# First-layer expert weights kept on chip, with a ScalarE copy per block in place of a transfer per block

## The chip, the core and the metric

The kernel runs on one core of one Trainium2 chip. The metric is the device time of one execution in microseconds (us), the median of the timed runs; lower is better. One further execution was recorded by the hardware profiler, and all rows below come from it.

## What is computed

Four layers, one after the other, on x of 64 samples x 32 tokens x 128 features, all in float32. The first one orthogonalises two matrices and adds a gated response. The second normalises the tokens and passes each through the two best of eight experts. The third passes each sample through one of eight experts, and the fourth rotates the features. The change is in the second layer, called the first expert layer here, since the one after it has experts too. Cut to what matters:

```python
# first expert layer: h_flat is [2048, 128], exp_w1 [8, 128, 512], exp_w2 [8, 512, 128]
probs = jax.nn.softmax(h_flat @ router_w, axis=-1)
gates, idx = jax.lax.top_k(probs, 2)
gates = gates / gates.sum(-1, keepdims=True)
hid = jax.nn.relu(jnp.einsum('nd,edf->nef', h_flat, exp_w1) + exp_b1)
eout = jnp.einsum('nef,efd->ned', hid, exp_w2) + exp_b2
y = jnp.einsum('ned,ne->nd', eout, combine)      # combine holds the two gates of a token
x = x + y.reshape(x.shape)
# second expert layer: one expert per sample
h = gelu(x @ Wi[expert] + bi[expert]);  o = h @ Wo[expert] + bo[expert];  y = layernorm(o + x) * gamma + beta
```

## The kernel before

Each engine runs its own instruction list, written out by hand, and waits on semaphores. The expert layers don't compute all eight experts for all tokens. The 4096 pairs of token and expert are sorted on the chip into NB1 = 39 blocks of 128 rows, each block of one expert. Which expert a block has is known only at run time: VectorE writes the table `bexi` (39 integers) and signals `places`. From then on an instruction that depends on the expert takes its address from a register, which that engine has loaded from the table (`value_load`: one load instruction and two range instructions, shown as ISA in the order of instructions).

For block b of the first expert layer:

- POOL gathers its 128 rows of h from memory into `hg` (L481, a ring of RING = 4 places; it waits until block b - 4 was transposed). From block 8 on, after every second of them, it also issues a gather `xg` for the second expert layer (L474), which waits for the one two before it. The six left over follow after block 38.
- TensorE transposes `hg` (L833), and VectorE copies the result to `hgT` (L1166).
- TensorE does the up product with the 128x512 matrix `ws[r]`, r = b mod 4 (L837, four matmuls, each in two passes). This waits for `hgT`, for the matrix (`w1_ready`) and for the hidden step of block b - 2.
- ScalarE does the bias and Relu of one half of the hidden columns (L620), VectorE that of the other half (L1174).
- TensorE does the down product with `w2`, which holds all eight experts on chip (L857). The expert is in a register.
- VectorE adds the expert's output bias, `b2blk[r]`, into `es` (L1184, two places), and SP stores `es` to memory (L364).

TensorE works staggered: in step b it does the transpose of block b + 2, the up product of b + 1 and the down product of b. VectorE does the copy of b + 2, the hidden half of b + 1 and the output add of b.

SP's queue brings the matrices in. Its step b is the store of block b, then a register load, then the transfer of the matrix of block b + 4 into `ws[r]` (L356, 256 KB), then that of the bias row, spread to all partitions (L359, 64 KB). The store waits for the output add of block b, and so do the transfers behind it.

When all blocks are stored and all x gathers have landed, POOL starts the gathers of the second expert layer (L498). That layer has NB2 = 22 blocks and uses the same ring `ws` for its matrices; `wo`, `g2r` and `be2r` stay on chip. VectorE and ScalarE hold the experts of its blocks in registers (`expert2`). They load them one by one during the late blocks of the first layer: VectorE after the output adds from block 15 on (L1160, L1199), ScalarE after hidden steps (L624).

## Time and profile before

| | |
|---|---|
| median of 3 runs | 327.73 us (327.21 to 332.39) |
| span of the profiled execution | 321.2 us |
| TensorE busy in it (matmul / weight load) | 77% / 61% |
| VectorE, ScalarE, POOL busy | 57%, 35%, 40% |
| chain that ended last | PE 53%, DVE 16%, DMA 10%, POOL 8%, issue 8% |
| ws transfers of the first expert layer (L356) | 39 of 256 KB, median 3.4 us from issue to landing |
| b2blk transfers (L359) | 39 of 64 KB, median 3.8 us |
| es stores (L364) | 39 of 64 KB, median 3.8 us |
| DMA traffic in the first expert layer | about 200 GB/s |

How to read it: the span goes from the first to the last instruction on the core; the timed runs also hold what lies around it. PE is TensorE's matmul side, PEld its weight-load side, DVE VectorE, ACT ScalarE, POOL GpSimd, SP the engine that issues most transfers (SPq: its queue). Register instructions and waits don't count as busy. In a row such as `[0.38 <-issue]` the engine was idle for 0.38 us before the instruction, and what ended that was nothing that the profile shows ("issue"), or the engine and line named. Granted clock (PEclk) is the share of TensorE's full clock that it was given. Up to about 105 us the kernel runs the first layer and the normalisation, up to 138 us it routes and sorts, from 138 to 239 us the first expert layer's blocks run, and from there the second one's.

### The profile page before, as it was taken

What the parts mean: (1) busy time and instruction counts of PE and PEld (TensorE: products, weight loads), DVE (VectorE), ACT (ScalarE), POOL (GpSimd) and SP (SyncE); (2) the same over time, 40 slices, a digit from 0 to 9 for tenths busy, and PEclk for the clock granted to TensorE, in tenths of its full rate; (3) what the DMA queues carried; (4) which work ended last, traced back from release to release, by engine and by line L of the source; (5) the groups of instructions that cost most, each with busy time, mean ns of one, the idle gap of its engine ahead of it and who ended that gap; (6) DMA issues with size and microseconds to landing.
All of it is one profiled execution on the core that took longest, in us unless ns stands there. A gap on an engine that the chain in (4) does not pass through costs nothing.

```text
span 321.2 us, 6590 instructions
## 1 busy us (share of the span) xinstructions
PE 247.4 (77%) x1630; PEld 195.3 (61%) x1630; DVE 184.2 (57%) x828; ACT 113.0 (35%) x393; POOL 129.6 (40%) x169
## 2 busy tenths in 40 slices
PE   4999999997548742888888859786843997998950
PEld 2656566445424632487778859786832886887840
DVE  1456656524989699244444525453522587897982
ACT  3343354225273313022222312221212664665640
POOL 6000000000152108465556535565347787778410
PEclk9999999955755655699999998999995999999985
DMA  5169600000050045237787775866745555656200
GB/s 140 27 168 317 177 2 0 1 2 0 0 132 0 2 131 161 30 75 210 199 204 192 205 200 144 184 200 189 201 106 152 152 150 152 171 132 161 75 24 19
DMA packets 38266, 38.42 MB, mean 120 GB/s; under 512 B 9491, under 2 KB 25909, under 8 KB 38230
## 3 DMA queue, kind: packets, MB, share of 16 engines
q1 hardware_dynamic: 32038, 26.18, 29.5%
q0 software_dynamic: 3360, 7.02, 10.8%
q10 hardware_dynamic: 2832, 4.80, 5.0%
q8 instruction: 15, 0.25, 0.3%
q14 instruction: 21, 0.17, 0.2%
HBM read 32.18 MB, written 6.19 MB: 119 GB/s over the span
## 4 chain that ended last, share of the span: by engine, by line
PE 53%; DVE 16%; DMA 10%; POOL 8%; issue 8%; ACT 2%; DVEq 0%; SPq 0%; ACTq 0%; POOLq 0%
PE bank L837 15%; PE bank L857 11%; PE bank L717 10%; DMA big<-expert_rows,xg 7%; PE bank L725 5%; POOL big L498 5%; PE bank L896 2%; PE bank L743 2%; DMA expert_rows<-es 2%; POOL ohp L451 2%; DVE x1r L1038 1%; DMA hg<-h_rows,map 1%; DVE bst L1043 1%; PE bank L893 1%; PE bank L833 1%
## 5 line engine op out<-in xcount | busy, mean ns | idle before, releaser
L837 PE MATMUL bank<-hgT,ws 128*128 128x128 f32 x488 | 68.5, 285 | 16.4 <-issue 9.9
L837 PEld LDWEIGHTS bank<-hgT,ws 128*128 128x128 f32 x488 | 61.2, 197 | 21.7 <-issue 13.4
L620 ACT ACTIVATE hid<-bank,bh 128x128 f32<-128x128 f32 x78 | 24.4, 364 | 84.4 <-PE bank L837 83.1
L481 POOL DMA_INDIRECT hg<-h_rows,map x39 | 37.0, 949 | 38.0 <-PE bank L833 30.9
L717 PE MATMUL bank<-ones 128*128 128x512 bf16 x176 | 49.2, 415 | 3.5 <-ACT trs L517 3.5
L498 POOL DMA_INDIRECT big<-expert_rows,xg x44 | 42.8, 973 | 15.0 <-issue 11.5
L857 PE MATMUL bank<-w,hid 128*128 x312 | 42.3, 279 | 0.3
L1174 DVE TENSOR_SCALAR hid<-bank,bh 128x128 f32<-128x128 f32 x78 | 23.8, 347 | 30.7 <-PE bank L837 30.6
L857 PEld LDWEIGHTS bank<-w,hid 128*128 128x128 f32 x312 | 38.6, 194 | 0.7 <-issue 0.7
L438 POOL TENSOR_SCALAR big<-x1r,rstd,nmr 128x128 f32<-128x128 f32 x8 | 3.5, 447 | 80.7 <-DVE nmr L1053 80.7
L717 PEld LDWEIGHTS bank<-ones 128*128 128x128 bf16 x176 | 18.9, 119 | 20.8 <-issue 5.9
L725 PEld LDWEIGHTS bank<-Q 128*128 128x128 f32 x128 | 19.3, 210 | 18.1 <-DVE Q L981 10.6
L648 ACT ACTIVATE hid<-bank,bh 128x128 f32<-128x128 f32 x88 | 25.2, 369 | 8.0 <-PE bank L837 7.5
L569 ACT ACTIVATE gsn<-bank 128x1 f32<-128x1 f32 x64 | 11.0, 171 | 43.5 <-PE bank L725 42.1
L896 PE MATMUL bank<-wo,hid 128*128 x176 | 25.5, 288 | 0.0
L474 POOL DMA_INDIRECT xg<-x_rows,map x22 | 20.8, 944 | 11.6 <-DMA xg<-x_rows,map 6.1
L725 PE MATMUL bank<-Q 128*128 128x32 f32 (+31 forms) x128 | 21.1, 280 | 5.2 <-DMA Q<-in_L_cond_V_dram 3.3
L977 DVE RECIPROCAL gsr<-gsd 128x2 f32<-128x2 f32 x32 | 5.3, 165 | 32.8 <-ACT gsd L574 32.7
L896 PEld LDWEIGHTS bank<-wo,hid 128*128 128x128 f32 x176 | 21.3, 191 | 2.7
L1166 DVE COPY hgT<-bank 128x128 f32<-128x128 f32 x39 | 11.2, 287 | 15.1 <-issue 9.5
L1184 DVE TENSOR_TENSOR es<-bank,b2blk 128x128 f32<-128x128 f32 x39 | 11.4, 292 | 14.3 <-PE bank L857 12.4
L1225 DVE SCALAR_TENSOR_TENSOR x2a<-big,xg 128x128 f32<-128x128 f32 x22 | 7.7, 349 | 18.3 <-DMA big<-expert_rows,xg 18.3
(260 smaller groups left out, 363.8 us busy)
## 6 DMA issues: line engine op xcount, KB each, us to landing
ws<-in_L_cond_exp_w_dram SPq DMA_DIRECT2D x39, 256.0 KB, 3.4
ws<-in_L_cond_Wi_dram ACTq DMA_DIRECT2D x18, 256.0 KB, 3.1
b2blk<-in_L_cond_exp_b_dram SPq DMA_DIRECT2D x39, 64.0 KB, 3.8
expert_rows<-es SPq DMA_DIRECT2D x39, 64.0 KB, 3.8
out_dram<-yo SPq DMA_DIRECT2D x80, 16.0 KB
x_rows<-x1r SPq DMA_DIRECT2D x1, 1024.0 KB, 6.9
h_rows<-big SPq DMA_DIRECT2D x4, 256.0 KB, 2.4
ws<-in_L_cond_Wi_dram SPq DMA_DIRECT2D x4, 256.0 KB, 3.9
```

The lines of the kernel that those rows point to most:

```text
L474: pool.indirect_dma_start(out=xg[:, j, :], out_offset=None, in_=xdram, in_offset=bass.IndirectOffsetOnAxis(ap=map2[:, j:j + 1], axis=0)).t ...
L481: pool.indirect_dma_start(out=hg[:, b % RING, :], out_offset=None, in_=hdram, in_offset=bass.IndirectOffsetOnAxis(ap=map1[:, b:b + 1], axi ...
L498: pool.indirect_dma_start(out=eg[:, j, k, :], out_offset=None, in_=edram, in_offset=bass.IndirectOffsetOnAxis(ap=xg[:, j, C_SLOT + k:C_SLO ...
L620: last = act.activation(hid[:, u, c, :], ps[2 + u][:, c * P:(c + 1) * P], ACT.Relu, bias=bh1[:, c, b:b + 1])
L648: last = act.activation(hid[:, u, c, :], ps[2 + 2 * (c // 2) + u][:, c % 2 * P:(c % 2 + 1) * P], ACT.Gelu, bias=bh2[:, c, j:j + 1])
L717: mm(ps[bank][:], ones[:], ones[:].unsqueeze(1).to_broadcast([P, 4, P]), start=True, stop=True)
L725: mm(ps[4 * k][:, 0:R - i], Q[:, k, i:i + 1].to_broadcast([P, P]), Q[:, k, i:R], start=True, stop=True).then_inc(gs_dots, 1)
L837: last = mm(ps[2 + 2 * (c // 2) + u][:, c % 2 * P:(c % 2 + 1) * P], ws[:, w, c * P:(c + 1) * P], hgT[:, u, :], start=True, stop=True)
L857: last = mm(ps[6 + u][:, 0:D], hid[:, u, c, :], w2[:, bass.ds(e, 1), c, :], start=(c == 0), stop=(c == FC - 1))
L896: last = mm(ps[6 + u][:, 0:D], hid[:, u, c, :], wo[:, bass.ds(e, 1), c, :], start=False, stop=(c == FC - 1))
L1174: last = dve.tensor_scalar(hid[:, u, c, :], ps[4 + u][:, (c - FC // 2) * P:(c - FC // 2 + 1) * P], bh1[:, c, b:b + 1], 0.0, ALU.add, ALU.max)
L1184: dve.tensor_tensor(es[:, u, :], ps[6 + u][:, 0:D], b2blk[:, r % RING, :], ALU.add).then_inc(es_ready, 1)
```

## The change

The kernel after loads `exp_w1` of all eight experts (2 MB) into `w1` and all rows of `exp_b2`, spread over the partitions (512 KB), into `b2r`, once, on SP's queue after the other weights and ahead of `wo`. In place of the transfer per block, ScalarE copies the matrix of block b + 3 from `w1` to `ws`, right after its hidden step of block b; the first three copies come before block 0. VectorE reads the bias row straight from `b2r`. SP only stores in this stage. The expert numbers are now needed in registers of ScalarE and VectorE. They are loaded in batches: blocks 0 to 19 before the stage, 20 to 38 in the middle of it, and those of the second layer at its end (22 on VectorE, 18 on ScalarE). The register loads one by one are gone. Everything else is the same; the instructions of POOL and TensorE are unchanged.

```diff
+        w1 = sb("w1", [P, E, FF])
+        b2r = sb("b2r", [P, E, D])
-        b2blk = sb("b2blk", [P, RING, D])
...
+        def experts_in(table, first, last, engine):
+            _, es_ = nc.values_load_multi_w_load_instructions(table[0:1, first:last], engines=[engine], min_val=0, max_val=E - 1)
+            return list(es_)
+        def row_of(t, e):
+            return t[:, bass.ds(e, 1), :].rearrange("p o d -> p (o d)")
...
+            sp.dma_start(w1[:], exp_w1.rearrange("e d f -> d e f")).then_inc(ld_w1, 16)
+            sp.dma_start(b2r[:], exp_b2.partition_broadcast(P)).then_inc(ld_w1, 16)
             sp.dma_start(wo[:], Wo.rearrange("e (c p) d -> p e c d", p=P)).then_inc(ld_wo, 16)
...
-            def weights1(b, r):
-                e = sp.value_load(bexi[0:1, b:b + 1], min_val=0, max_val=E - 1)
-                if b >= RING:
-                    sp.wait_ge(up_ps, b - RING + 1)
-                sp.dma_start(ws[:, r, :], exp_w1[bass.ds(e, 1), :, :].rearrange("e d f -> (e d) f")).then_inc(w1_ready[r], 16)
-                if b >= RING:
-                    sp.wait_ge(es_ready, b - RING + 1)
-                sp.dma_start(b2blk[:, r, :],
-                             exp_b2[bass.ds(e, 1), :].rearrange("e d -> (e d)").partition_broadcast(P)).then_inc(b2_ready[r], 16)
-            def step1(b, r):
-                store(b, r)
-                if b + RING < NB1:
-                    weights1(b + RING, r)
-            sp.wait_ge(places, 1)
-            for b in range(RING):
-                weights1(b, b)
-            blocks(NB1, step1)
+            blocks(NB1, store)
...
                 last.then_inc(hidA_sb, 1)
-                if 0 <= b - FIRST2 < NB2 - RING:
-                    expert2.append(act.value_load(bex2i[0:1, RING + b - FIRST2:RING + b - FIRST2 + 1], min_val=0, max_val=E - 1))
+                if b + RING - 1 < NB1:
+                    weights1(b + RING - 1, (r + RING - 1) % RING)
+            def weights1(b, r):
+                if b >= RING:
+                    act.wait_ge(up_ps, b - RING + 1)
+                act.activation(ws[:, r, :], row_of(w1, expert1[b]), ACT.Copy).then_inc(w1_ready, 1)
...
-            blocks(NB1, hidden)
+            act.wait_ge(places, 1)
+            act.wait_ge(ld_w1, 32)
+            expert1 = experts_in(bexi, 0, 20, mybir.EngineType.Activation)
+            for b in range(RING - 1):
+                weights1(b, b)
+            for b in range(20 - RING + 1):
+                hidden(b, b % RING)
+            expert1 += experts_in(bexi, 20, NB1, mybir.EngineType.Activation)
+            for b in range(20 - RING + 1, NB1):
+                hidden(b, b % RING)
+            expert2 += experts_in(bex2i, RING, NB2, mybir.EngineType.Activation)
...
-                pe.wait_ge(w1_ready[r % RING], 16 * (b // RING + 1))
+                pe.wait_ge(w1_ready, b + 1)
...
-                dve.wait_ge(b2_ready[r % RING], 16 * (b // RING + 1))
-                dve.tensor_tensor(es[:, u, :], ps[6 + u][:, 0:D], b2blk[:, r % RING, :], ALU.add).then_inc(es_ready, 1)
+                dve.tensor_tensor(es[:, u, :], ps[6 + u][:, 0:D], row_of(b2r, expert1[b]), ALU.add).then_inc(es_ready, 1)
...
-                if 0 <= b - FIRST2 < NB2:
-                    expert2.append(expert(bex2i, b - FIRST2))
+            dve.wait_ge(ld_w1, 32)
+            expert1 = experts_in(bexi, 0, 20, mybir.EngineType.DVE)
...
-            blocks(NB1, step1)
+            for b in range(20):
+                step1(b, b % RING)
+            expert1 += experts_in(bexi, 20, NB1, mybir.EngineType.DVE)
+            for b in range(20, NB1):
+                step1(b, b % RING)
+            expert2 = experts_in(bex2i, 0, NB2, mybir.EngineType.DVE)
```

ScalarE's queue at the beginning of the stage, from the copies of the bias tables (`bh`) to the first hidden steps, before:

```order
L632 ACTIVATE bh<-bank 128x156
L633 ACTIVATE bh<-bank 128x88
L620 ACTIVATE hid<-bank,bh 128x128 x32
L624 TENSOR_LOAD bex2i
L624 ISA x2
L620 ACTIVATE hid<-bank,bh 128x128 x2
```

And after, where L611 is the hidden step and L620 the copy into the ring:

```order
L628 ACTIVATE bh<-bank 128x156
L629 ACTIVATE bh<-bank 128x88
L307 TENSOR_LOAD bexi
L307 ISA x40
L620 ISA
L620 ACTIVATE ws<-w 128x512
...
L611 ACTIVATE hid<-bank,bh 128x128 x2
L620 ISA
L620 ACTIVATE ws<-w 128x512
```

A load of 20 values with its 40 range instructions and three copies now stand between the bias tables and the first hidden step, and each hidden step (two instructions) is followed by one address instruction and one copy.

The same queue in mid stage, after: the second batch stands between the copy for block 19 and the hidden step of block 17. Before, there was nothing but hidden steps and single loads.

```order
L620 ACTIVATE ws<-w 128x512
L307 TENSOR_LOAD bexi
L307 ISA x38
L611 ACTIVATE hid<-bank,bh 128x128 x2
L620 ISA
L620 ACTIVATE ws<-w 128x512
```

Nothing of the batch's length may pass the hidden step behind it, for which TensorE's down product of block 17 waits.

VectorE's queue in mid stage, before, at a late block, with the output add (L1184), the single load (L1160), the copy of hgT (L1166) and the hidden half (L1174):

```order
L1184 TENSOR_TENSOR es<-bank,b2blk 128x128
L1160 TENSOR_LOAD bex2i
L1160 ISA x2
L1166 COPY hgT<-bank 128x128
L1174 TENSOR_SCALAR hid<-bank,bh 128x128 x2
```

And after, behind the output add of block 19:

```order
L1186 ISA
L1186 TENSOR_TENSOR es<-bank,b2r 128x128
L307 TENSOR_LOAD bexi
L307 ISA x38
L1169 COPY hgT<-bank 128x128
L1177 TENSOR_SCALAR hid<-bank,bh 128x128 x2
```

One load with 38 range instructions now stands ahead of the copy of hgT for block 22, at one place, and each output add has an address instruction ahead of it.

## Rows read from the trace of the kernel before

**Rows 1.** Timeline, ScalarE's hidden steps: start us, us, engine, line, operation [idle before <-releaser].
```profile
142.38 0.63 ACT L620 ACTIVATE hid<-bank,bh 128x128 f32<-128x128 f32 x2 [1.67 <-PE bank L837]
144.27 0.62 ACT L620 ACTIVATE hid<-bank,bh 128x128 f32<-128x128 f32 x2 [1.27 <-PE bank L837]
...
234.66 0.63 ACT L620 ACTIVATE hid<-bank,bh 128x128 f32<-128x128 f32 x2 [1.59 <-PE bank L837]
```

**Rows 2.** Timeline, a stretch without a hole, 225.4 to 227.1 us.
```profile
225.41 0.62 ACT L620 ACTIVATE hid<-bank,bh 128x128 f32<-128x128 f32 x2 [1.28 <-PE bank L837]
...
226.10 0.97 PEld L837 LDWEIGHTS bank<-hgT,ws 128*128 128x128 f32 x8
...
226.30 0.29 DVE L1184 TENSOR_TENSOR es<-bank,b2blk 128x128 f32<-128x128 f32 x1 [0.28 <-PE bank L857]
...
226.99 0.97 PEld L857 LDWEIGHTS bank<-w,hid 128*128 128x128 f32 x8
```

**Rows 3.** Waits of TensorE's load side, 138 to 238: us in total, times, longest.
```profile
PEld bank L837 <- issue: 13.4, 17, 2.7
PEld bank L837 <- DVE hgT L1166: 8.0, 7, 1.9
```

**Rows 4.** Timeline, the transfer for block 4 and its up product.
```profile
142.78 0.35 SPq L356 DMA_DIRECT2D ws<-in_L_cond_exp_w_dram  x1
...
145.62 1.13 PE L837 MATMUL bank<-hgT,ws 128*128 128x128 f32 x8 [0.38 <-issue]
```

**Rows 5.** Groups by shape, ScalarE: xcount | busy us, mean ns | idle before.
```profile
L522 ACT ACTIVATE big<-big 128x512 f32<-128x512 f32 x4 | 2.4, 615 | 0.0
```

**Rows 6.** Timeline, VectorE: output add and next copy, without and with a load.
```profile
174.51 0.29 DVE L1184 TENSOR_TENSOR es<-bank,b2blk 128x128 f32<-128x128 f32 x1 [0.28 <-PE bank L857]
174.72 0.28 DVE L1166 COPY hgT<-bank 128x128 f32<-128x128 f32 x1
...
182.40 0.29 DVE L1184 TENSOR_TENSOR es<-bank,b2blk 128x128 f32<-128x128 f32 x1 [0.28 <-PE bank L857]
...
183.10 0.29 DVE L1166 COPY hgT<-bank 128x128 f32<-128x128 f32 x1 [0.41 <-issue]
```

**Rows 7.** Timeline, VectorE and ScalarE at the beginning of either expert layer.
```profile
137.54 0.73 DVE L1166 COPY hgT<-bank 128x128 f32<-128x128 f32 x2 [5.46 <-PE bank L833]
...
139.42 1.29 ACT L620 ACTIVATE hid<-bank,bh 128x128 f32<-128x128 f32 x4 [12.94 <-PE bank L837]
...
244.62 0.35 DVE L1225 SCALAR_TENSOR_TENSOR x2a<-big,xg 128x128 f32<-128x128 f32 x1 [7.46 <-DMA big<-expert_rows,xg]
```

**Rows 8.** Timeline, the last output add and the second layer's first gather.
```profile
236.86 0.29 DVE L1184 TENSOR_TENSOR es<-bank,b2blk 128x128 f32<-128x128 f32 x1 [1.01 <-PE bank L857]
...
238.96 0.94 POOL L498 DMA_INDIRECT big<-expert_rows,xg  x1 [2.88 <-DMA expert_rows<-es]
```

**Rows 9.** Groups by shape, POOL, 138 to 238 us.
```profile
L474 POOL DMA_INDIRECT xg<-x_rows,map x22 | 20.8, 944 | 11.6 <-DMA xg<-x_rows,map 6.1 <-issue 5.5
```

**Rows 10.** Landings: es in 194:199, hg in 150:160, hg in 140:143.
```profile
DMA to landing us min/median/max: 1.7/1.7/1.7
...
DMA to landing us min/median/max: 3.9/4.1/4.3
...
DMA to landing us min/median/max: 2.5/2.5/2.5
```

**Rows 11.** Stretches: length, PE, PEld, DVE, ACT, POOL busy, PEclk, DMA share, GB/s.
```profile
192.00:194.00 2.00, 2.00 (x11) 2.00 (x11) 0.59 (x3) 0.03 (x1) 0.74 (x1) 0.50 0.18 54
194.00:199.00 5.00, 5.00 (x43) 5.00 (x42) 2.66 (x10) 1.52 (x6) 2.42 (x4) 0.90 0.58 154
```

**Rows 12.** TensorE after its longest hole: a timeline row, then rows of the chain.
```profile
190.23 1.13 PE L837 MATMUL bank<-hgT,ws 128*128 128x128 f32 x8 [2.47 <-issue]
...
191.36 1.41 PE bank L857 x8
...
192.98 1.71 PE bank L837 x8
```

More of the change, by code:

```diff
@@ L265, in cond_seq_kernel @@
         SHARED = 4
-        FIRST2 = NB1 - NB2 - 2
         RESP_BANK = (1, 2, 5, 6)
@@ L269, in cond_seq_kernel @@
         N_SMALL, N_ROWS, N_CONST, N_SIDE = len(SMALL), len(ROWS), 17 + len(IOTAS), TILES + 6
-        (ld_uv, ld_x, ld_small, ld_w2, ld_wo, ld_rows, consts, act_own, dve_own, gs_dots, gs_root, gs_norm,
+        (ld_uv, ld_x, ld_small, ld_w2, ld_w1, ld_wo, ld_rows, consts, act_own, dve_own, gs_dots, gs_root, gs_norm,
          q_ready, xt_ps, xt_sb, pooled_ps, sid_ready, side_ps, side_sb, crow_ready, fold_ps, fold_sb,
@@ L280, in cond_seq_kernel @@
          ve2_ready, rs2_ready, yn_ready, yo_ready, c_x2a, b_rr, b_stats, b_aggr, n_yg, n_yb, n_rot) = map(sem, """
-         ld_uv ld_x ld_small ld_w2 ld_wo ld_rows consts act_own dve_own gs_dots gs_root gs_norm q_ready
+         ld_uv ld_x ld_small ld_w2 ld_w1 ld_wo ld_rows consts act_own dve_own gs_dots gs_root gs_norm q_ready
          xt_ps xt_sb pooled_ps sid_ready side_ps side_sb crow_ready fold_ps fold_sb style_exp z_exp
@@ L293, in cond_seq_kernel @@
         eg_ready = [sem(f"eg_ready{i}") for i in range(RING)]
-        w1_ready = [sem(f"w1_ready{i}") for i in range(RING)]
-        b2_ready = [sem(f"b2_ready{i}") for i in range(RING)]
+        w1_ready = sem("w1_ready")
         wi_ready = [sem(f"wi_ready{i}") for i in range(RING)]
@@ L1156, in _ @@
                             ps[3][:, 2 * P:3 * P].rearrange("p (k i) -> p i k", i=TILES)).then_inc(x_row_ready, 1)
-            def expert(table, b):
-                return dve.value_load(table[0:1, b:b + 1], min_val=0, max_val=E - 1)
             def columns(b, r):
```

3 lines of the change are left out of this document (removed).

## Prediction, made before the changed kernel ran

> **What bounds the kernel now.** I started with the table of stretches and the waits, since the change touches one stage, the 39 first-layer expert blocks. ScalarE's third hidden step (block 2) starts at 142.38 and its last (block 38) at 234.66 [rows 1]. So 36 blocks take 92.28 us, 2.56 us each. Yet block 2 to block 3 takes 1.89 us (142.38 to 144.27) [rows 1]. In a late stretch TensorE's weight loads follow each other without a hole, up at 226.10, down at 226.99, 0.89 us a leg [rows 2]: two legs and a transpose of 0.11 make 1.89 us, TensorE's own pace. 36 × (2.56 − 1.89) = 24.2 us are lost to something.
>
> The waits of TensorE's load side say where: before L837, the up product, 13.4 us with no releaser that the profile shows and 8.0 us put down to VectorE's copy of hgT [rows 3]. No other wait of that size is in the list. The name of VectorE misleads. The copy just before such a stall is that of the block after next; the copy which up needs was done a block earlier. What is left of up's conditions is `w1_ready`, a DMA, and the times fit: SP issues the matrix of block 4 at 142.78, behind the store of block 0, and up of block 4 starts at 145.62 after an idle 0.38 us, 2.84 us after the issue [rows 4]. The ring has four places, but the issue waits for block 0's output add, so the transfer has less than two blocks to land in. At 1.89 us a block it does not. [...]
>
> **What goes.** 39 transfers of 256 KB and 39 of 64 KB leave the stage. What up waits for becomes a ScalarE copy from SBUF. A plain ACTIVATE of 128x512 f32 from SBUF to SBUF takes 0.615 us [rows 5]. ScalarE has 0.63 us of hidden work per block, starting 0.2 us after up ends [rows 2]; with the copy and its one address instruction it comes to about 1.3 of 1.89 us. Block b's copy is issued right after the hidden step of block b − 3, so it is done some 1.3 us after up of b − 3, and up of b starts two periods later: more than 3 us to spare. Gain: **24.2 us**, provided that nothing else then sets the pace.
>
> **What is added.** (a) One load of 2 MB and one of 512 KB before `wo`, in the first 60 us. At the table's rates it is some 10 us of transfer; it lands long before block 0 and nothing but the second layer's `wo` is behind it. Cost 0; without cover at most those 10 us.
>
> (b) Register loads: a block's expert number must be in a register of ScalarE and of VectorE. They come in batches of 20, 19 and (22 or 18): one load instruction plus two range instructions a value. The trace has single loads, on VectorE after each output add of a late block: from the start of the add to the start of the next copy 174.51 to 174.72 = 0.21 us without, 182.40 to 183.10 = 0.70 us with a load [rows 6]; 0.49 us for one load and two register instructions. How that splits is not shown. Bounds for a register instruction: nothing, and 0.118 us, since TensorE's queue gets through 16 instructions (nine matmuls, one load, six register instructions) in 1.89 us [rows 2]. I take 0.08, so the load itself is 0.33.
>
>  - Before block 0: 20 values, 0.33 + 40 × 0.08 = 3.5 us. VectorE is idle 5.46 us there and ScalarE 12.94 us, of which three copies take 1.9 [rows 7]. Hidden. Between the layers VectorE is idle 7.46 us for 22 values, 3.9 us [rows 7]. Hidden.
>  - In mid stage: 19 values, 0.33 + 38 × 0.08 = 3.4 us on each engine. On VectorE it stands ahead of the copy of hgT for block 22. In the steady rows the add starts at 226.30 and the up after next would start at 226.10 + 1.89 = 227.99; less 0.29 for the copy and 0.1 for the signal leaves 1.3 us of slack [rows 2]. Stall 2.1 us. On ScalarE it stands ahead of hidden of block 17: the hidden step shown begins at 225.41, the one before 1.89 us earlier, and the copy is handed over some 0.6 us into that, at 224.1; the step shown has to begin by 226.2 to be ready for the down product at 226.99 [rows 2]; slack 2.1, stall 1.3 us. They hit different blocks, so they add up: **3.4 us**. Behind each stall stand only hidden steps and copies, which TensorE waits for itself.
>
> (c) The end. The second layer's gathers begin when the last output store has landed (2.1 us after the last add, [rows 8]) and when all x gathers have. Six x gathers are left after block 38's h gather, and each waits for the one two before it; POOL issues at 0.944 + 0.30 us each [rows 9]. With a landing of l us the last has landed 2.4 + 4l us after the transpose of block 34. At 1.89 us a block the store has landed 14.6 us after it. A gather's landing is 4.1 us (median of a loaded stretch) and 2.5 us at its lightest [rows 10]; at 4.1 the x chain would end 4.2 us late, at 3.3 it would be 1.0, at 2.5 nothing. The stage loses two thirds of its bytes, so I take between the last two: **0.5 us**.
>
> [...]
>
> (d) TensorE's clock. [...]
>
> **Sum.** 24.2 − 3.4 − 0.5 = 20.3 us. The profiled span of 321.2 becomes 300.9; the median of the runs is 6.5 us above the span, so 327.7 becomes **307.4 us**. The second layer (from 239.0) is shifted, not changed: its preloads, its gathers and its SP queue stand as before.
>
> **Rivals.**
>  1. *Forecast*, 305 to 311 us. Chance 0.55.
>  2. *The loads hide.* If a register instruction costs next to nothing (the batch stays near 0.5 us), both are inside the slack, and the tail too: 327.7 − 24.2 = 303.5. For it: TensorE carries a load and six register instructions per block without a hole [rows 2]. Against: VectorE's 0.49 is visible. Chance 0.15.
>  3. *POOL becomes the pace.* From block 8 on it issues three gathers per two blocks, 3 × 1.244 = 3.73 of 3.78 us [rows 9]. If waiting for its semaphores stretches the pitch to 1.4 us, 31 blocks go at 2.1 instead of 1.89: 6.5 us more, 313.9. Or the store of es, double-buffered, binds: landing + 0.44 us per two blocks, which needs over 3.3 us; 1.7 at lighter load speaks against it [rows 10]. Chance 0.15.
>  4. *The change does not do what it says*: up did not wait for ws but for something that comes as late (the h gather, say). Then only part is gained, within 2%, 321.2 or more. Against: no wait before the transpose L833 in the list [rows 3]. Chance 0.05.
>  5. *Slower: register loads at full single price.* If each value costs 0.49 us also in a batch, the first batch is 9.8 − 5.46 = 4.3 us late on VectorE; mid stage 9.3 − 1.3 = 8.0 and 9.3 − 2.1 = 7.2; between the layers 10.8 − 7.46 = 3.3 [rows 6, 7, 2]. With two clock drops (2.6) and the tail (0.5) 25.9 us: 329.4. It decides from about 0.46 us a value. Against: a batch has one load instruction, not 20, and register instructions are under 0.118 on TensorE. It is 5 us off 2% slower. Chance 0.06; 0.04 are left for what I don't see.
>
> **Numbers.** The upper bound of the known terms: 0.33 + 38 × 0.118 = 4.8 us a batch, stalls 3.5 + 2.7 = 6.2, two clock drops 2.6, tail 4.2, so a gain of 11.2 and 316.5; all at once is unlikely. Range **303 to 315**, which leaves about 2 in 10 out. Two per cent is 6.6 us, about what a measurement of this kernel can tell from no change. Faster by more: cases 1 to 3 and most of the unseen, 0.88. Within: case 4, most of 5, 0.09. Slower: 0.03.
>
> **What would show it.** Right: hidden steps 1.89 us apart; no "issue" wait before up; DMA share in the stage near 0.4; last es add near 216.5; one hole of about 1.3 us at block 17 (ScalarE) and one of about 2 at block 20 to 22 (VectorE); first gather of the second layer near 219. The split of register cost is read from these holes: above 4.8 us for a batch the bound was wrong. If L833 shows waits for hg, rival 3. The prediction falls if the period stays above 2.1 us with ws copied long before.

## The result, and the profile after

| | before | after |
|---|---|---|
| median of the timed runs | 327.47 us (326.07 to 332.39, 4 runs) | 321.08 us (316.72 to 322.54, 4 runs) |
| span of the profiled execution | 321.2 us | 314.5 us |
| first to last output add of the first expert layer | 141.4 to 236.9 us | 145.3 to 228.9 us |
| ScalarE busy | 35% | 42% |

The changed kernel is faster: ratio 0.9718, 95% interval 0.9636 to 0.98. That ratio leaves out executions more than 1.5% above the fastest of their kernel, two of the changed kernel's four among them; by the medians of the table it is 0.98. The forecast was 307.4 us and a range of 303 to 315, so the direction was right and the size wrong, by 13.7 us. Of the 20.3 us forecast, the spans show 6.7 (321.2 − 314.5) and the medians 6.4.

In the code after, L843 is the up product (L837 before), L863 the down product (L857), L839 the transpose (L833), L611 the hidden step and L620 the ring copy on ScalarE, L1169 the copy of hgT, L1177 VectorE's hidden half, L1186 the output add, L307 the register loads and their range instructions.

First a table of stretches of the kernel after, with the columns of [rows 11].

```profile
150.00:160.00 10.00, 10.00 (x92) 10.00 (x91) 6.02 (x22) 6.24 (x18) 7.46 (x8) 1.00 0.39 94
160.00:170.00 10.00, 10.00 (x92) 10.00 (x92) 5.57 (x21) 6.23 (x17) 7.54 (x8) 1.00 0.40 90
170.00:180.00 10.00, 6.68 (x60) 6.50 (x59) 4.39 (x16) 3.33 (x10) 5.66 (x6) 1.00 0.30 75
180.00:190.00 10.00, 6.75 (x60) 6.51 (x59) 2.49 (x9) 4.64 (x13) 5.66 (x6) 1.00 0.25 62
190.00:200.00 10.00, 7.44 (x41) 7.44 (x42) 3.40 (x13) 2.29 (x6) 2.22 (x3) 0.66 0.10 27
200.00:210.00 10.00, 10.00 (x92) 10.00 (x91) 5.60 (x21) 5.92 (x16) 7.11 (x8) 1.00 0.32 83
```

Where nothing stands in the way, TensorE is busy 10.00 of 10.00 us, with 90 GB/s of transfers beside it. Between 170 and 200 it is not, and in 190 to 200 the granted clock averages 0.66. The waits of 138 to 230, with the columns of [rows 3], say on what:

```profile
DVE hgT L1169 <- issue: 14.7, 2, 7.7
PEld bank L843 <- DVE hgT L1169: 8.2, 2, 6.0
...
ACT hid L611 <- issue: 5.2, 1, 5.2
...
PEld bank L863 <- issue: 3.5, 1, 3.5
```

The 13.4 us of "issue" waits before up, and the seven waits of up to 1.9 us put down to hgT [rows 3], are gone. In their place stand two long waits on VectorE, one on ScalarE, and the holes that they make on TensorE: 6.0 and 2.2 us before up, 3.5 before down. The timeline shows what each engine did before. VectorE before block 0, then VectorE in mid stage, then ScalarE in mid stage and TensorE behind the two holes (columns as in [rows 1]):

```profile
132.21 0.29 DVE L1161 COPY x1r<-bank 128x128 f32<-128x128 f32 x1 [0.25 <-PE bank L831]
140.22 0.49 DVE L1169 COPY hgT<-bank 128x128 f32<-128x128 f32 x2 [7.72 <-issue]
...
184.89 0.29 DVE L1186 TENSOR_TENSOR es<-bank,b2r 128x128 f32<-128x128 f32 x1 [0.39 <-PE bank L863]
192.21 0.29 DVE L1169 COPY hgT<-bank 128x128 f32<-128x128 f32 x1 [7.03 <-issue]
...
173.25 0.63 ACT L620 ACTIVATE ws<-w 128x512 f32 x1
179.04 0.62 ACT L611 ACTIVATE hid<-bank,bh 128x128 f32<-128x128 f32 x2 [5.16 <-issue]
...
179.79 0.97 PEld L863 LDWEIGHTS bank<-w,hid 128*128 128x128 f32 x8 [3.50 <-issue]
...
192.56 2.07 PE L843 MATMUL bank<-hgT,ws 128*128 128x128 f32 x8 [5.81 <-DVE hgT L1169]
194.42 1.91 PE L863 MATMUL bank<-w,hid 128*128 x8
```

Between the two VectorE instructions of each pair, and between the two of ScalarE, the engine's queue holds one register load and its range instructions and nothing else of length. The chain of work that ended last goes through them and shows them one by one. Its columns are start us, us, what; DVEq and ACTq are the engines' sequencers. First the start of the mid-stage batch on VectorE, then a piece of the one on ScalarE:

```profile
185.19 1.68 DVEq L307
186.90 0.19 DVEq L307
187.18 0.19 DVEq L307
187.46 0.18 DVEq L307
187.73 0.18 DVEq L307
...
191.86 0.18 DVEq L307
192.21 0.30 DVE hgT L1169
```

```profile
172.85 0.51 ACTq L307
173.36 0.52 ACT ws L620
173.88 0.83 issue
174.70 0.15 ACTq L307
...
176.06 0.15 ACTq L307
176.28 0.15 ACTq L307
```

On VectorE the load of 19 values takes 1.68 us, and after it one value follows another every 0.275 us (186.90, 187.18, 187.46, 187.73): two range instructions, 0.14 us each on average. (The chain has a long row of 0.18 and a short one of 0.02 for each value, with gaps between them, so the two are not alike; the pair is what counts.) 1.7 + 19 × 0.275 = 6.9 us; 7.0 from add to copy. On ScalarE the first range instruction stands 1.85 us behind the load's start (172.85 to 174.70), and one value follows another every 0.22 us, 0.11 an instruction on average: 1.85 + 19 × 0.22 = 6.0 us of the 6.2 from 172.85 to 179.04. The forecast had 3.4 us for each batch.

**Accounts.** Before minus after, from the adds, the first gather of the second layer (238.96 and 231.06), its first x2a (244.62 and 237.33) and the end: the stage itself 95.5 − 83.6 = 11.9 us shorter; its first add 3.9 later, of which 0.5 because routing ended later in this execution (the table `map` at 131.76 in place of 131.3), about 0.3 because the first gather landed later behind it, and the rest, 3.1, because of the first batch; from last add to first gather 0.1 longer (2.2 in place of 2.1), from gather to x2a 0.6, from there to the end 0.6. 11.9 − 3.9 − 0.1 − 0.6 − 0.6 = 6.7. And within the stage: 38 periods of 1.895 us, less 0.8 at the end, where the last two adds stand 1.1 apart, are 71.2 of the 83.6. The other 12.4 are the holes of 3.5 and 6.0 us and the slow legs behind the second one: 2.07, 1.71, 1.71 and 1.02 us in the chain in place of 0.89 each, 3.0 us more.

### The profile page after: what moved, and what is told of

It is laid out like the page before. It is cut to its first block, busy times and chain, and to the rows that moved or that the text cites. A ratio compares the mean times of both kernels' runs of the same rounds, so it can differ in the third digit from the quotient of the medians.

```text
span 314.5 us, 6478 instructions
## 1 busy us (share of the span) xinstructions
PE 246.1 (78%) x1630; PEld 198.9 (63%) x1630; DVE 181.8 (58%) x828; ACT 132.9 (42%) x432; POOL 129.5 (41%) x169
## 4 chain that ended last, share of the span: by engine, by line
PE 58%; DVE 18%; DMA 6%; DVEq 6%; issue 5%; POOL 3%; ACT 2%; ACTq 1%; SPq 0%
PE bank L843 16%; PE bank L863 11%; PE bank L723 10%; DVEq L307 6%; PE bank L731 6%; DMA big<-expert_rows,xg 5%; PE bank L902 4%; PE bank L749 2%; POOL ohp L442 2%; PE bank L899 2%; DVE x1r L1044 1%; PE bank L839 1%; ACTq L307 1%; DVE bst L1049 1%; PE bank L799 1%
## 5 line engine op out<-in xcount | busy, mean ns | idle before, releaser
L843 PE MATMUL bank<-hgT,ws 128*128 128x128 f32 x488 | 70.6, 292 | 7.8 <-DVE hgT L1169 7.8
L843 PEld LDWEIGHTS bank<-hgT,ws 128*128 128x128 f32 x488 | 64.9, 207 | 8.2 <-DVE hgT L1169 8.2
L611 ACT ACTIVATE hid<-bank,bh 128x128 f32<-128x128 f32 x78 | 24.4, 364 | 49.8 <-PE bank L843 44.6
L863 PE MATMUL bank<-w,hid 128*128 x312 | 42.4, 280 | 3.3 <-ACT hid L611 3.3
L863 PEld LDWEIGHTS bank<-w,hid 128*128 128x128 f32 x312 | 39.1, 197 | 3.6 <-issue 3.5
L1177 DVE TENSOR_SCALAR hid<-bank,bh 128x128 f32<-128x128 f32 x78 | 23.8, 346 | 17.5 <-PE bank L843 17.5
L620 ACT ACTIVATE ws<-w 128x512 f32 x39 | 24.3, 628 | 6.1 <-issue 6.1
L1186 DVE TENSOR_TENSOR es<-bank,b2r 128x128 f32<-128x128 f32 x39 | 11.4, 291 | 21.7 <-PE bank L863 18.3
L1169 DVE COPY hgT<-bank 128x128 f32<-128x128 f32 x39 | 10.9, 282 | 14.7 <-issue 14.7
## 6 DMA issues: line engine op xcount, KB each, us to landing
w<-in_L_cond_exp_w_dram SPq DMA_DIRECT2D x1, 2048.0 KB, 11.2
```

The source lines that it names most:

```text
L611: last = act.activation(hid[:, u, c, :], ps[2 + u][:, c * P:(c + 1) * P], ACT.Relu, bias=bh1[:, c, b:b + 1])
L620: act.activation(ws[:, r, :], row_of(w1, expert1[b]), ACT.Copy).then_inc(w1_ready, 1)
L843: last = mm(ps[2 + 2 * (c // 2) + u][:, c % 2 * P:(c % 2 + 1) * P], ws[:, w, c * P:(c + 1) * P], hgT[:, u, :], start=True, stop=True)
L863: last = mm(ps[6 + u][:, 0:D], hid[:, u, c, :], w2[:, bass.ds(e, 1), c, :], start=(c == 0), stop=(c == FC - 1))
L1177: last = dve.tensor_scalar(hid[:, u, c, :], ps[4 + u][:, (c - FC // 2) * P:(c - FC // 2 + 1) * P], bh1[:, c, b:b + 1], 0.0, ALU.add, ALU.max)
```

## The experiments

The runs fell on four chips. On one of them the kernel before took 325.6 us, as on the chip of the result; on the three others it took 351 to 355. Ratios are therefore taken within one chip alone, and what sets these chips apart has its own part below. The time in the heading of a group is the median of the kernel before on its chip.

### First group (before: 355.17 us)

No range instructions, everything else as in the change. The table's values are clamped by VectorE when it writes them:

```diff
-            _, es_ = nc.values_load_multi_w_load_instructions(table[0:1, first:last], engines=[engine], min_val=0, max_val=E - 1)
+            _, es_ = nc.values_load_multi_w_load_instructions(table[0:1, first:last], engines=[engine], min_val=0, max_val=E - 1,
+                                                                  skip_runtime_bounds_check_because="the table is clamped to E - 1 by VectorE")
```

> The changed kernel without the two range instructions per loaded value; the batches of 20, 19 and 22 (18) values and all else stay. Theory A (the range instructions are the cost: in the changed kernel 38 of them take 5.3 us on VectorE, 185.19 + 1.68 to 192.21, and 5.7 us on ScalarE, so 0.14 to 0.15 us each, and the load instruction 1.68 and 0.51 us): a batch takes about 1.7 us on VectorE and 0.5 on ScalarE. The 3.5 us hole at the down product goes, the 6.0 us hole at the up product shrinks to 0.5 or less, the copy of hgT for block 0 starts right after its transpose, and TensorE's clock stays up: 316.7 minus (2.2 + 1.2 clock at the beginning, 3.5, 6.0 + 3.0 clock, 0.6 between the layers), plus 0.4, is about 301 us. Theory B (loading many values at once is slow whatever follows): the holes stay within 1 us of 3.5 and 6.0, and the time stays within 2 us of the changed kernel.

Single loads with range instructions, one per block on each engine, in place of the batches:

```diff
+                e = act.value_load(bexi[0:1, b:b + 1], min_val=0, max_val=E - 1)
+                act.activation(ws[:, r, :], row_of(w1, e), ACT.Copy).then_inc(w1_ready, 1)
...
+                if b + 1 < NB1:
+                    expert1.append(expert(bexi, b + 1))
+                if 0 <= b - FIRST2 < NB2:
+                    expert2.append(expert(bex2i, b - FIRST2))
```

> The changed kernel with one load per block instead of batches, range instructions kept: ScalarE loads a block's expert just ahead of the copy, VectorE after the output add of the block before; the second layer's loads stand one by one at the late blocks as in the kernel before. Theory A (a load with its two range instructions costs about 0.5 us on VectorE and is hidden as long as no more than the slack of 1.3 us is asked at a time, on ScalarE 2.1): no holes, hidden steps 1.89 us apart, last output add near 213, about 301 us. Rival (an engine's slack is used up by a load in each block, two in the late ones): the period grows to 2.0 or 2.1, 305 to 309 us, with holes before up put down to VectorE's copy.

The matrices on chip, but the bias rows again by a transfer of 64 KB per block, so that VectorE needs no expert numbers in the first expert layer:

```diff
-                dve.tensor_tensor(es[:, u, :], ps[6 + u][:, 0:D], row_of(b2r, expert1[b]), ALU.add).then_inc(es_ready, 1)
+                dve.wait_ge(b2_ready[r % RING], 16 * (b // RING + 1))
+                dve.tensor_tensor(es[:, u, :], ps[6 + u][:, 0:D], b2blk[:, r % RING, :], ALU.add).then_inc(es_ready, 1)
```

> The changed kernel with the bias rows brought in by a 64 KB transfer per block as before (b2blk, four places), so VectorE needs no expert numbers in the first layer and its batches of 20 and 19 go; ScalarE's copies and batches stay, also VectorE's batch of 22 between the layers. Theory A: the holes due to VectorE go (2.2 + 1.2 at the beginning, 6.0 + 3.0 in mid stage), the hole of 3.5 us at ScalarE's batch stays: 316.7 - 12.4 = about 304 us. Rival (the 64 KB transfers with their stores are in the way: SP's queue or the landings bind): the period stays above 2.0 us and the time above 308.

The kernel before, with the transfer of the matrix issued ahead of the store on SP's queue:

```diff
                 if b >= RING:
-                    sp.wait_ge(es_ready, b - RING + 1)
+                    store(b - RING, r)
...
-                store(b, r)
                 if b + RING < NB1:
                     weights1(b + RING, r)
+                else:
+                    store(b, r)
```

> The kernel before with one thing moved: SP issues the matrix transfer of block b + 4 as soon as block b's up product is done, ahead of the store of block b instead of behind it, some 1.6 us earlier in the steady state. Nothing is kept on chip. Theory A (TensorE waited for a transfer that was issued too late, 2.84 us ahead of its need against a landing of 3.4): the waits before the up product mostly go, period 1.9 to 2.0 us, 307 to 311 us. Rival (the DMA traffic itself binds, about 200 GB/s now and 270 at TensorE's pace): landings grow to 4.5 us or more, the period stays above 2.3, over 318 us.

| kernel | us | ratio to before, 95% | output adds, first to last |
|---|---|---|---|
| x1 no range instructions | 345.46 | 0.974, 0.9627 to 0.9854 | 142.5 to 229.8 |
| x2 single loads | 349.16 | 0.9818, 0.9724 to 0.9911 | 143.2 to 232.0 |
| x3 bias by transfer | 351.08 | 0.9833, 0.9718 to 0.9949 | 146.6 to 238.5 |
| x4 before, early issue | 351.1 | 0.9877, 0.9779 to 0.9976 | 145.4 to 241.4 |

In absolute numbers all four missed, since the chip was another. Their intervals overlap, so the times alone do not rank them; the traces say more. In x3 VectorE has no batch left, and no wait of "issue" kind before its hgT copy is in the list of 138 to 240 us, where the changed kernel has two of up to 7.7 us; ScalarE kept its batch, and its longest wait of that kind before a hidden step is 5.8 us, against 5.2. So each hole goes with the batch of its own engine. In x2, with a load in every block, the longest "issue" wait before hgT is 1.0 us: spread over the blocks, the same instructions make no long hole. x4 kept 15.2 us of "issue" waits before up, so the order on SP's queue alone doesn't bring the matrix in time.

### Second group (before: 352.92 us)

The changed kernel itself and the one without range instructions (same edits as above), on another chip:

> The changed kernel, unaltered, beside the next two, since the four runs before this one were taken where the kernel before needs 355 us instead of 327, and so don't stand beside it. Theory A (its three holes cost 13 to 16 us over x1): it lies 10 to 16 us above the run without range instructions. Theory B (the holes are made up for elsewhere): within 5 us of it.

> The changed kernel without range instructions again, beside the changed kernel. Theory A: 10 to 16 us faster than it, and about 0.92 to 0.95 of the kernel before. Theory B: less than 5 us faster.

VectorE with one load per block, also without range instructions; ScalarE keeps its batches:

```diff
+                if b + 1 < NB1:
+                    expert1.append(expert(bexi, b + 1))
...
+            def expert(table, b):
+                return experts_in(table, b, b + 1, mybir.EngineType.DVE)[0]
+            expert1, expert2 = [expert(bexi, 0)], []
-            expert1 += experts_in(bexi, 20, NB1, mybir.EngineType.DVE)
```

> As the run without range instructions, and VectorE's batches replaced by one load per block (second layer's loads one by one at the late blocks): what is left of its holes should be the load instructions of 1.68 us before block 0 (hidden), at block 20 (0.4 to 1.4 us) and between the layers (hidden). Theory A: 0.5 to 1.5 us faster than without range instructions. Rival (a single load per block, at the late ones two, costs VectorE more than it saves): 1 to 3 us slower than that.

The changed kernel with ScalarE's mid-stage batch issued twice:

```diff
             expert1 += experts_in(bexi, 20, NB1, mybir.EngineType.Activation)
+            experts_in(bexi, 20, NB1, mybir.EngineType.Activation)
```

> The changed kernel with ScalarE's mid-stage batch (one load, 38 range instructions) issued twice in a row. Theory A (the hole at the down product is the batch's length less the slack; a batch is 0.51 + 5.68 = 6.2 us): ScalarE's hidden step of block 17 begins about 11.3 us instead of 5.2 us late, and the hole before the down product is 3.5 + 6.2 = 9.7 us; VectorE's hole stays as it was. Rival (the hole has another cause, an instruction fetch or a signal): it grows by 1 us or less.

| kernel | us | ratio to before, 95% | output adds |
|---|---|---|---|
| y1 changed | 363.55 | 1.0282, 1.0208 to 1.0355 | 144.9 to 246.3 |
| y2 no range instructions | 345.69 | 0.972, 0.9602 to 0.9838 | 144.0 to 232.6 |
| y3 the same, VectorE single | 344.89 | 0.9764, 0.9693 to 0.9834 | 142.8 to 233.3 |
| y4 ScalarE's batch twice | 373.03, one run | | |

The range instructions are worth 18 us here. y1 and y4 fell on the kind of chip described below, so a part of their waits is not the batches'. The doubled batch tests the mechanism: the waits of y1, then of y4 (there the lines of TensorE are one higher), same columns as above:

```profile
ACT hid L611 <- remote: 37.2, 15, 3.3
...
PEld bank L863 <- issue: 15.7, 15, 4.7
DVE hgT L1169 <- issue: 14.8, 2, 7.7
```

```profile
PEld bank L864 <- issue: 21.6, 15, 10.4
DVE hgT L1170 <- issue: 14.4, 2, 7.7
...
ACT hid L611 <- issue: 11.2, 1, 11.2
```

ScalarE's hole becomes 11.2 us, and TensorE's longest wait before the down product goes from 4.7 to 10.4, by 5.7 us for one batch more (6.2 was expected, the batch's own length); VectorE's waits stay. So the batch is the hole.

### Third group (before: 351.61 us)

The kernel before, for its trace on such a chip; the changed kernel; the one of y3; and that one with a load per block on ScalarE too (an edit as in x2, without range instructions):

> The kernel before, for its trace. On the chips of the last two comparisons it took 352 to 355 us, on the first one 327.7, and no trace of it was taken there. If this chip is of the slower kind: theory A (signals from TensorE to the other engines come some 1.2 us late, in both expert layers) expects the first expert layer to be longer than on the first chip (first to last output add 95.7 us there) by less than the changed kernel's, since up waits for the transfer anyway: 97 to 101 us; and the second layer, from its first gather to the end, 100 to 106 us in place of 82.2. Theory B (the DMA alone is slower there) expects the issue wait before up to be above 30 us in place of 13.4 and 8.0, and the signals as fast as before. If it is of the faster kind, the rows are those known and the time is 327 us.

> The changed kernel again, beside a trace of the kernel before. On a chip where before takes 327 us: 321 us, ratio 0.97 to 0.98. On one where it takes 353: the ratio was 1.028 on one such chip; theory A (late signals add to the length of each register batch and to the start-up behind it) expects 1.02 to 1.03 again; if the result is under 1.00, the slower result was that one chip's.

> No range instructions anywhere; VectorE loads one number after each output add, ScalarE still in batches of 20 and 19. Price of range instructions (theory A): on a chip of the faster kind 14 to 17 us below the changed kernel, 304 to 308 us, which is what the prediction's sum came to with batches that hide. On a chip of the slower kind 345, as before, 16 to 19 us below changed. Rival: the rest of the forecast gain was lost to something else than the batches (the ring copies on ScalarE, signals); then not below 312 on the faster kind.

> As the kernel before it in this call, but ScalarE too loads one number before each ring copy, without range instructions, so that no batch stands in the first expert layer on either engine. A load of one value without range instructions was 0.2 us on VectorE. ScalarE then has 0.65 of hidden step, 0.2 to 0.5 of load and 0.63 of copy, at most 1.8 of 1.89 us. If the load is 0.2, the time is the same as with batches (within 1 us, since the batch of 19 values without range instructions left no hole at block 17). If a single load costs 0.5 us or more on ScalarE, its hidden steps come late and the time is 3 to 10 us longer.

Medians: z1 350.66 (one run), z2 360.73 (ratio 1.0203, 1.0055 to 1.0351), z3 348.87 (0.99, 0.9835 to 0.9966), z4 347.51 (0.99, 0.9858 to 0.9941). So the changed kernel came out slower on a second chip too, though with an interval that reaches down to 0.55%. z3 and z4 can't be told apart by these times: a single load fits into ScalarE's period as well as a batch without range instructions does. z3 was expected at 345 and 16 to 19 us below z2; it came to 3.9 us above the first number and 11.9 below z2.

### Fourth group (before: 325.58 us)

The same three kernels on a chip of the kind that the forecast was for:

> The changed kernel, as the base for the two below. If before takes 327 us here: 316 to 322 us. If it takes some 350, signals from TensorE come late in both expert layers, the period is 2.31 us in place of 1.89, and the changed kernel takes 355 to 363 us.

> The changed kernel without range instructions, batches kept. My theory (range instructions at 0.14 to 0.15 us each are the whole hole behind a batch): where before takes 327 us, the holes of 3.5 us (block 17) and 6.0 us (block 22), the late start (2.2), what the clock costs behind them (1.2 and 3.0) and 0.6 between the layers go, all but some 1.4 of the middle hole: 302 to 306 us, and the first to the last output add in 73 to 76 us. Rival (the forecast gain was lost to something else too): 308 to 314. Where before takes 350 us: 345, the adds in 87 to 89 us.

> As the one before it, but VectorE loads one value after each output add. Expected: no hole in mid stage at all, 0 to 2 us below it on a chip of the first kind, equal within 1 us (or up to 3 us above, as on the last chip) on the other.

| kernel | us | ratio to before, 95% | span | output adds |
|---|---|---|---|---|
| w1 changed | 318.69 | 0.9819, 0.9755 to 0.9883 | 317.6 | 146.1 to 231.1 |
| w2 no range instructions | 308.86 (302.8 to 310.61) | 0.9541, 0.9451 to 0.9631 | 300.6 | 142.5 to 214.9 |
| w3 the same, VectorE single | 303.42 (300.46 to 304.88) | 0.9325, 0.9228 to 0.9422 | 302.7 | 146.3 to 217.4 |

Stretches of w2, then of w3, columns as in [rows 11]:

```profile
170.00:180.00 10.00, 10.00 (x92) 10.00 (x92) 5.19 (x19) 6.23 (x18) 7.41 (x9) 1.00 0.35 90
180.00:190.00 10.00, 8.98 (x81) 8.74 (x80) 5.59 (x21) 5.09 (x14) 6.57 (x7) 1.00 0.31 82
190.00:200.00 10.00, 10.00 (x92) 10.00 (x92) 5.82 (x22) 6.10 (x17) 7.54 (x8) 1.00 0.36 93
```

```profile
180.00:190.00 10.00, 10.00 (x93) 10.00 (x92) 5.70 (x22) 6.23 (x17) 7.50 (x8) 1.00 0.36 92
```

In w2 one hole is left, behind the load of the 19 values on VectorE; the chain and the timeline of w2 there:

```profile
179.17 1.73 DVEq L307
```

```profile
PEld bank L844 <- DVE hgT L1170: 1.7, 2, 1.3
```

Without range instructions the batch is 1.73 us, against a slack forecast at 1.3. The longer of TensorE's two waits is 1.3 us; the add before this batch also began late, behind a store that landed late (`[0.79 <-DMA expert_rows<-es]`), so that not all of the 1.3 is the load's: the add came at 178.88, some 0.4 us behind its turn (1.9 us after the one at 176.59). In w3 the stage has no hole between its first and last add, and its adds take 71.1 us, the 71.2 of a stage without holes. That w3's span is 2.1 us longer than w2's all the same comes from ahead of the stage: routing ended at 134.3 in w3's execution and at 132.3 in w2's, and the first add is 3.8 later.

w1 less w2, by span: 317.6 − 300.6 = 17.0 us, made of 3.6 at the start, 12.6 in the stage (85.0 against 72.4), 0.4 to the first gather and 0.4 behind it. So in the profiled executions the whole of the missing gain was in the range instructions: the span of 300.6 us is what the sum of the prediction came to (300.9). By medians less of it is shown. w1 less w2 is 9.8 us, w1 less w3 15.3. w2's own median came out at 308.86, above the 302 to 306 expected; its profiled execution took 302.8 and the three others 307.42 to 310.61, which have no trace, so what they lost stays open. w3 has the lowest median on this chip, 22.2 us below the kernel before; y3 and y2, on a chip of the other kind, can't be told apart.

## Chips on which signals come late

On three chips the kernel before takes 351 to 355 us, and on the two of them where the changed kernel ran it is 2 to 3% slower. The traces show where. Output adds (VectorE) of before in z1, and the first gather of the second layer (POOL) in the same trace: count, ns, first and last start.

```profile
L1184 DVE TENSOR_TENSOR es<-bank,b2blk x39: 280/292/293, 142.7 to 239.2; 128x128 f32<-128x128 f32 x39
```

```profile
L498 POOL DMA_INDIRECT big<-expert_rows,xg x44: 942/954/1167, 241.3 to 325.6; - x44
```

Before's first expert layer takes 96.5 us there, nearly the 95.5 of the forecast's chip. It is the second layer that is long, from its first gather to the end of the span (348.4) 107.1 us in place of 82.2. The changed kernel (y1) has 110.2 us there, and w1 83.7, so the second layer costs both kernels about 25 us more on such a chip.

In the first expert layer the traces of these chips do not hold 1.89 us a block. ScalarE in y1, in a stretch without batches:

```profile
156.00 0.63 ACT L611 ACTIVATE hid<-bank,bh 128x128 f32<-128x128 f32 x2 [2.49 <-remote]
156.51 0.63 ACT L620 ACTIVATE ws<-w 128x512 f32 x1
157.03 0.62 ACT L611 ACTIVATE hid<-bank,bh 128x128 f32<-128x128 f32 x2
157.53 0.64 ACT L620 ACTIVATE ws<-w 128x512 f32 x1
160.68 0.63 ACT L611 ACTIVATE hid<-bank,bh 128x128 f32<-128x128 f32 x2 [2.50 <-remote]
```

Two hidden steps come close together, then nothing for 2.5 us: two blocks in 4.68 us and, over the 38 periods of y2 (144.0 to 232.6), 2.33 a block. The releaser is one that the profile can't name ("remote"). The up product that this step needs begins at 153.24. In the trace of after the hidden step follows 1.10 us behind such a start (150.78 to 151.88); here it is 2.76, so 1.7 late. VectorE's half of the same step begins at the same moment, 156.00, and TensorE has gone on to its next products at 154.13 and 155.13. Both halves wait for one signal, TensorE's, and it is read here as coming late; since the profile models the ends of matmuls, that is an inference. The next down product of TensorE then waits 0.6 to 0.8 us. With it the signs of the result can be accounted for:

 - before needs 2.56 us a block for its transfers and hides the 2.33; with the change 36 × (2.56 − 2.33) = 8.3 us remain to be gained in place of 24.2;
 - the batches cost as much as on the other kind (14.8 us of waits before hgT in y1 and w1, 5.6 and 5.1 before hidden; y1 less y2 is 12.8 us from first to last add, w1 less w2 12.6), so the sum turns negative: y1's adds take 101.4 us against 96.5 of before;
 - without range instructions the adds take 88.6 us (y2), 7.9 less than before, near the 8.3.

These sums set z1 beside y1 and y2, which ran on another chip of the same kind. On z1's own chip the adds of z3 and z4 take 92.4 and 89.8 us, some 4 and 7 less than before, so the 8.3 is not reached there. And the stage is not the whole of the loss: by span y1 is 10.2 us above z1, 4.9 of it in the stage, 2.2 ahead of it and 3.1 behind the first gather of the second layer (110.2 against 107.1), of which no row here shows the cause.

Why this happens on these chips, and only there, stays open. No experiment touched it. Theory B of z1's expectation (the DMA alone is slower) is refuted: the "issue" wait before up is 18.7 us in z1, not above 30, and with the 2.8 put down to hgT it is 21.5 us, near the 13.4 + 8.0 = 21.4 of the forecast's chip [rows 3]. Theory A missed both its ranges by little: 96.5 us for the first layer in place of 97 to 101, 107.1 for the second in place of 100 to 106.

## Why the prediction was right or wrong

**What bounds the kernel: right.** The transfer of the matrix was the 2.56 us. With it gone, the up and down products (legs) stand 0.89 us apart in the stretches without a batch, and no wait of "issue" kind before up is left. The chain after:

```profile
150.95 0.89 PE bank L843 x8
151.84 0.89 PE bank L863 x8
152.84 0.89 PE bank L843 x8
```

**What goes: right.** The ring copy takes 629 ns (36 of them, 22.6 us, with no idle before them), 615 was taken from [rows 5]. It hides. DMA share 0.39 and 0.40, "near 0.4".

**(a) The load of 2.5 MB: right.** The stages up to the table are as before but for 0.5 us. That is within what executions differ by: the table comes at 131.2 to 134.4 us in the traces with the load, and at 131.3, 131.5 and 133.9 in the three without it.

**(b) Register loads: the step that failed.** Three terms were mis-sized. The range instruction was taken as 0.08 us with 0.118 as the bound; it is 0.14 on VectorE and 0.11 on ScalarE, the mean of a pair. The bound came from TensorE's queue [rows 2] and did not hold for another engine. The load was taken as 0.33 us whatever its size: what was left of the 0.49 of a single one. It is 1.68 us for 19 or 20 values on VectorE, and 1.85 to the first range instruction on ScalarE. And the single price was split wrongly. In w3 add and copy (VectorE, timeline) stand 0.44 us apart with one load and no range instruction between them, 0.23 more than the 0.21 without [rows 6]. So of the 0.49, the load adds 0.23 and a range instruction 0.13:

```profile
161.42 0.29 DVE L1188 TENSOR_TENSOR es<-bank,b2r 128x128 f32<-128x128 f32 x1 [0.39 <-PE bank L865]
161.86 0.29 DVE L1171 COPY hgT<-bank 128x128 f32<-128x128 f32 x1 [0.15 <-issue]
```

 Had the split been 0.23 and 0.13, a batch of 19 would have come to 5.2 us with the load's size left out, and 6.6 with it. So VectorE's batch was 7.0 us in place of 3.4 and its hole 6.0 in place of 2.1; ScalarE's was 6.2, its hole 3.5 in place of 1.3. The two slacks were right. Counted as the forecast counts them, from the start of the add, and from 0.6 us into the hidden step ahead of the batch (172.73 + 0.6), they are 192.21 − 184.89 − 6.0 = 1.3 us and 179.04 − 173.33 − 3.5 = 2.2, with 1.3 and 2.1 forecast. Places and mechanism were right: blocks 17 and 22, hidden step and hgT copy, nothing else behind them. So the step that failed is the price of a batch, 3.4 us where 7.0 and 6.2 were measured.

**"Hidden" before block 0 and between the layers: wrong by the same step.** VectorE is idle 5.46 us before the stage [rows 7] and the batch took 7.7, so the first hgT copy came at 140.22 and up at 140.57 with 137.89 before; 2.2 us beyond the later end of routing (0.3 of them the later landing of the gather), and then 1.2 more in slow legs (2.08 and 1.40). The batch between the layers cost 0.6 us.

On VectorE the long load also took less than as many short ones would. A load of one value adds 0.23 us, and that of 20 values (132.50 in the chain of after) takes 1.68, 0.084 a value. Nineteen loads of one value would be 19 × 0.23 = 4.4 us, an estimate; the load of the mid-stage batch took 1.68 for its 19 (185.19 in the chain), and the range instructions the rest of the 7.0.

**(c) The tail: right in size.** From the last add to the first gather it is 2.2 us in after, 2.4 in w2 and 2.8 in w1 and w3, against 2.1 before [rows 8]: 0.1 to 0.7, 0.5 taken. Landings of hg are 2.5 us in the median of the stage in after, with 71 GB/s of traffic (138 to 229), and were 3.9 in before, with 180 GB/s (138 to 239).

**(d) The clock: the bound was the value.** 1.3 us for each drop was the bound and 0 was taken. The 1.3 is what the down and up legs behind the hole of 2.47 us in before took beyond 0.89 each, 1.41 and 1.71 us [rows 2, 12], with the granted clock at 0.50 in 192 to 194 [rows 11]. No run shows the 2.6 us that the prediction's sums carry for two drops: in mid stage one drop came in after, and it cost 3.0; two came in w1, which cost 1.3 and 2.9 (legs of 2.07, 1.71, 1.71 and 1.00 from 194.82 on). The drop in after stands behind the hole of 5.81 us, where the granted clock averages 0.66 over 190 to 200 (0.50 from 192 to 198). Behind ScalarE's hole of 3.50 us it stayed 1.00 (170 to 190), though it had fallen to 0.50 after 2.47 us before. That held in the one execution only. In w1, the same kernel, the same hole, also 3.5 us, was followed by slow legs; the chain there:

```profile
180.68 2.07 PE bank L863 x8
182.75 0.21 PE bank L839
182.96 1.24 PE bank L843 x8
```

The granted clock averages 0.57 over 180 to 184 in w1, and the two adds behind the hole come 1.3 us later than in after (8.7 us for two periods, 7.4 in after). So the bound of 1.3 us for this drop was paid in one execution and not in the other. In the traces of before, after and w1 each drop in mid stage stands behind a hole: 0.50 behind 2.47 us in before, 0.50 behind 5.81 in after, 0.57 behind 3.5 and 0.61 (192 to 200) behind 5.8 in w1. That not every hole brings one is what these two executions add.

**Rivals.** The forecast's mechanism is what happened, with batches near the "full single price" of rival 5: 7.0 us / 19 = 0.37 us a value, below the 0.46 from which it said the sign would turn. It turned on chips of the other kind, at the same price, where by the account above the gain is 8.3 us and not 24.2: rival 5 had the right mechanism and did not see that the gain too could shrink. Rival 2 (the loads hide) is near what w3 reaches: 22.2 us below before by medians, 24.2 in the rival. Rival 3 fell: gathers kept up at 1.89 us; es waits for its landing are small (3.0 us in 4 waits, and in w2 3.2 in 4), and stayed without effect but for the one above.

**Range.** Its upper end was built from the 0.118 bound: with the batches measured, and its own slacks of 1.3 and 2.1, the stalls in mid stage come to 5.7 and 4.1, the start adds 2.2, the clock 4.2, the batch between the layers 0.6 and the tail 0.1: 24.2 − 16.9 = 7.3 us of gain. 6.7 was measured. The step from span to median was also too large: in every later run the time lies 2.2 us above the span of the same execution, and 6.5 was added, so the profiled execution of before was some 4 us faster than its kernel's median. Gains taken as median less median don't depend on it.

## What to carry to other kernels

A register load is not free because it is "only a register": here a load of 19 values and its 38 range instructions took 7.0 us on VectorE, 1.68 of them the load. Count the load by its values and every range instruction on its own, on the engine that carries them, and put the sum against the engine's slack at that place (1.3 us here). If the table is known to be in range, leave the range instructions out, which was worth 17.0 us of span between w1 and w2, and spread what is left over the blocks, as in w3, where TensorE is busy 70.00 of the 70 us from 147 to 217. A bound taken from one engine's queue need not bind another's: 0.118 us from TensorE's stood against 0.14 on VectorE. And when a change removes the longest wait of a loop, ask what the second longest would be if the chip were a little different: here, as the traces are read above, it decided the sign, with 2.33 us a block (y2) on a chip of the other kind where the forecast had 1.89.

## What the hardware showed that was not expected

 - Two range instructions a value take 0.275 us on VectorE and 0.22 on ScalarE. On VectorE a load of one value adds 0.23 us and one of 20 values takes 1.68. The work that stands behind them in the engine's queue waited for all of it: the copy of hgT 7.03 us on VectorE, the hidden step 5.16 on ScalarE (after).
 - The same program takes 326 us on one chip and 351 to 355 on three others. In y1, on one of these, ScalarE's and VectorE's hidden steps begin some 1.7 us late every second block (2.49 us idle before ScalarE's, 0.75 in after, where they are in time), and waits of that kind reach 2.6 us in x3 and z4 on the two others. And a change that is 2 to 3% faster on the one kind was 2 to 3% slower on two of the three others.
 - A hole of 3.50 us on TensorE left the granted clock at 1.00 in one execution of the changed kernel and was followed by 0.57 (180 to 184) in another; one of 2.47 us in the kernel before was followed by 0.50.
